# Pruned attention in one core of a Trainium2: the last scaling of the layer norm moved from VectorE to GpSimd, behind the root that is computed there

## The reference

```python
def _layernorm(x, axis=-1, eps=1e-05):
    m = jnp.mean(x, axis=axis, keepdims=True)
    v = jnp.var(x, axis=axis, keepdims=True)
    return (x - m) / jnp.sqrt(v + eps)

def _pruned_attention(q, k, v):
    B, H, S, _ = q.shape
    scores = jnp.einsum('bhqd,bhkd->bhqk', q, k) / math.sqrt(D_K)
    scores = jax.nn.softmax(scores, axis=-1)
    keep = int(S * PRUNE_KEEP)
    col_sum = jnp.sum(scores, axis=2)
    _, idx = jax.lax.top_k(col_sum, keep)
    mask = jnp.zeros((B, H, S), scores.dtype).at[jnp.arange(B)[:, None, None], jnp.arange(H)[None, :, None], idx].set(1.0)
    pruned = scores * mask[:, :, None, :]
    return jnp.einsum('bhqk,bhkd->bhqd', pruned, v)
...
x = _layernorm(x + _L0_attn_ref(x, ...))
x = _layernorm(x + _L0_xattn_ref(x, ctx_1024, ctx_1024, ...))
x = _layernorm(x + _L0_ffn_ref(x, ...))
```

## Time and profile before

| what | value |
|---|---|
| three executions | 2188.01, 2197.36, 2202.60 us, median 2197.36 |
| the profiled execution, its own time | 2182.38 us |
| its span, first to last instruction | 2180.6 us |
| granted TensorE clock, mean | 0.933 |
| the stage's loop, batches 2 to 7 | from about 485 us to 970 us of the span |
| the stage's last store | 1023.6 us |

### The profile page before, as it was taken

One profiled execution on the slowest core, in us unless ns is written; L12 is line 12 of the kernel. 1 busy time (PEld: TensorE's weight loads), 2 busy tenths in 40 slices (PEclk: granted clock), 3 DMA queues, 4 the chain that ended last, 5 costly groups with the idle time before them and its releaser, 6 DMA issues. The chain is left out here.

```text
span 2180.6 us, 28641 instructions
## 1 busy us (share of the span) xinstructions
PE 1880.1 (86%) x8625; PEld 1134.5 (52%) x8625; DVE 1300.3 (60%) x3113; ACT 959.1 (44%) x2451; POOL 609.9 (28%) x781
## 2 busy tenths in 40 slices
PE   7794857888888888884697899999879999999997
PEld 5452534444554454551565565666555656566553
DVE  2483437988988988983354121122266677766655
ACT  3231549988888888880232211111123232223220
POOL 2010005555555555551355000100143122211100
PEclk9897988999999999997666999999999999999999
DMA  5523752112112112202622333433321121100000
GB/s 193 231 87 99 248 183 65 46 54 67 56 54 66 55 54 60 61 20 73 203 92 91 98 109 132 138 123 130 107 77 59 34 63 44 30 15 25 10 10 20
DMA packets 166839, 184.51 MB, mean 85 GB/s; under 512 B 19620, under 2 KB 145819, under 8 KB 165696
## 3 DMA queue, kind: packets, MB, share of 16 engines
q1 hardware_dynamic: 159424, 158.57, 22.5%
q0 software_dynamic: 6144, 16.18, 2.4%
q10 hardware_dynamic: 1152, 8.39, 0.9%
HBM read 118.68 MB, written 58.72 MB: 81 GB/s over the span
## 5 line engine op out<-in xcount | busy, mean ns | idle before, releaser
L746 POOL TENSOR_SCALAR xa_probs<-xa_probs,xa_rinv 128x512 f32<-128x512 f32 x512 | 344.6, 692 | 294.6 <-DVE xa_rinv L791 294.6
L911 PE MATMUL xa_ps_t<-xa_ident,xa_probs 128*128 128x128 f32 x2048 | 325.7, 285 | 60.8 <-POOL xa_probs L746 55.0
L764 ACT ACTIVATE xa_probs<-xa_ps_s,xa_nmax 128x512 f32<-128x512 f32 x512 | 351.9, 708 | 25.8 <-DVE xa_nmax L795 25.4
L911 PEld LDWEIGHTS xa_ps_t<-xa_ident,xa_probs 128*128 128x128 f32 x2048 | 232.4, 143 | 240.1 <-POOL xa_probs L746 84.7
L795 DVE TENSOR_REDUCE xa_nmax<-xa_ps_s 128x2 f32<-128x1024 f32 x256 | 307.3, 1201 | 39.5 <-PE xa_ps_s L903 38.0
L681 ACT ACTIVATE xa_probT<-xa_ps_t 128x512 f32<-128x512 f32 x368 | 226.5, 621 | 63.0 <-PE xa_ps_t L911 54.1
L2268 PE MATMUL ta_ps_e<-k_ew,ta_x5T 128*128 128x512 f32 x512 | 244.2, 613 | 1.5 <-DVE ta_acc L2018 1.4
L903 PE MATMUL xa_ps_s<-xa_k,xa_q 96*128 96x512 bf16 x512 | 157.8, 391 | 54.9 <-ACT xa_probs L764 34.5
L2018 DVE SCALAR_TENSOR_TENSOR ta_acc<-ta_ps_e,ta_gate,ta_acc 128x256 f32<-128x256 f32 x256 | 123.5, 482 | 101.7 <-PE ta_ps_e L2268 95.5
L1459 ACT ACTIVATE ex_hid<-ex_ps_g 128x512 f32<-128x512 f32 x64 | 38.2, 598 | 274.1 <-PE ex_ps_u L1561 274.1
L1515 DVE TENSOR_TENSOR ex_hid<-ex_hid,ex_ps_u 128x512 f32<-128x512 f32 x64 | 44.0, 687 | 182.0 <-ACT ex_hid L1459 182.0
(11 more groups left out here) (356 smaller groups left out, 2935.2 us busy)
## 6 DMA issues: line engine op xcount, KB each, us to landing
xa_q<-scratch_qk_parts SPq DMA_DIRECT2D x192, 64.0 KB, 2.2
xa_k<-scratch_qk_parts SPq DMA_DIRECT2D x192, 64.0 KB, 2.2
scratch_buf<-rec_zeros ACTq DMA_DIRECT2D x8, 1024.0 KB, 12.0
k_wg<-in_L_ffn_Wg SPq DMA_DIRECT2D x16, 512.0 KB, 5.8
k_wu<-in_L_ffn_Wu SPq DMA_DIRECT2D x16, 512.0 KB, 6.0
k_wd<-in_L_ffn_Wd SPq DMA_DIRECT2D x16, 512.0 KB, 6.7
ex_xs<-scratch_buf SPq DMA_DIRECT2D x16, 512.0 KB, 4.9
scratch_results<-ex_out SPq DMA_DIRECT2D x16, 512.0 KB, 3.3
```

The source lines that it names most:

```text
L746: ins = pool.tensor_scalar(probs[h % NP][:, t, :], probs[h % NP][:, t, :], rinv[h % 2][:, t:t + 1], 1.0, ALU.mult, ALU.mult)
L764: ins = act.activation(probs[h % NP][:, t, :], ps_s[j][:, t % 2, :], ACT.Exp, bias=nmax[h % 2][:, t:t + 1], accum_out=rsum[h % 2][:, t:t + 1])
L911: ins = pe.transpose(ps_t[t % 2][:, i * P:(i + 1) * P], probs[(h - 2) % NP][:, i, t * P:(t + 1) * P], ident[:, :])
```

## The change

`finish` leaves DVE's queue and stands in POOL's, in the same slot (half 0, slot 2), ahead of the head's scaling of that slot, behind a wait for POOL's own `root`. SP's store waits for a new semaphore `x2_up` that POOL raises, and the counter `ln`, which DVE raised four times a batch, is raised three times. At the end of the stage `finish` stands behind `root` in POOL's queue.

```diff
-            x_ld, x2_st = r.sem("x_ld"), r.sem("x2_st")
+            x_ld, x2_st, x2_up = r.sem("x_ld"), r.sem("x2_st"), r.sem("x2_up")
...
             def store(b):
-                sp.wait_ge(ln, 4 * b + 4)
+                sp.wait_ge(x2_up, b + 1)
                 sp.dma_start(tok(a["x2"][b]), x_in[:, :, :]).then_inc(x2_st, 16)
...
             def root(b):
-                pool.wait_ge(ln, 4 * b + 3)
+                pool.wait_ge(ln, 3 * b + 3)
                 pool.tensor_tensor(rstd[:, :], ve[:, :], mhalf[:, :], ALU.pow).then_inc(rstd_up, 1)
+
+            def finish(b):
+                pool.wait_ge(rstd_up, b + 1)
+                apart(pool, past_pool)
+                for t in range(T):
+                    ins = pool.tensor_scalar(x_in[:, t, :], x_in[:, t, :], mv[:, t, 0:1], rstd[:, t:t + 1], ALU.subtract, ALU.mult)
+                ins.then_inc(x2_up, 1)
...
                     if (u, h) == (0, 1) and since(b, 2):
                         root(b - 2)
+                    if (u, h) == (0, 2) and since(b, 2):
+                        finish(b - 2)
                     if real:
                         pool.wait_ge(rinv_up, n + 1)
...
             root(B - 1)
+            finish(B - 1)
...
                     if (u, h) == (0, 0) and since(b, 2):
                         stats(b - 2)
-                    if (u, h) == (0, 2) and since(b, 2):
-                        finish(b - 2)
-
-            def finish(b):
-                dve.wait_ge(rstd_up, b + 1)
-                for t in range(T):
-                    ins = dve.tensor_scalar(x_in[:, t, :], x_in[:, t, :], mv[:, t, 0:1], rstd[:, t:t + 1], ALU.subtract, ALU.mult)
-                ins.then_inc(ln, 1)
             batches(dve, body)
             stats(B - 1)
-            finish(B - 1)
```

More of the change, by code:

```diff
@@ L833, in stats @@
                 ins.then_inc(ln, 1)
-                dve.wait_ge(ln, 4 * b + 1)
+                dve.wait_ge(ln, 3 * b + 1)
                 apart(dve, past_dve)
@@ L838, in stats @@
                 ins.then_inc(ln, 1)
-                dve.wait_ge(ln, 4 * b + 2)
+                dve.wait_ge(ln, 3 * b + 2)
                 dve.tensor_scalar(ve[:, :], mv[:, :, 1], 1e-5, None, ALU.add).then_inc(ln, 1)
```

## The result

The changed kernel took 2209.72 us (median of 4 runs, 2207.23 to 2224.03); the kernel before took 2193.01 us beside it (4 runs, 2188.01 to 2202.6). The ratio is 1.0092, with a 95% interval of 1.0047 to 1.0138: some 20 us slower, between 10 and 30. The forecast was 2195.6 us in a range of 2185 to 2204, so the change came out on the other side and outside the range.

A forecast was written before the change was run, and what follows sets the result against it. DVE was taken as the fullest engine (91%), with PE's turned sums close behind finish. Six passes at 0.33 us gave -2.0, the stage's end +0.2: -1.8 us, so 2195.6 us against the median 2197.36, range 2185 to 2204.

The forecast's parts named there:

- the gain is 7.95 - 7.62 = 0.33 us a pass: Half 0, DVE up to the copy of the turned sums: without finish it becomes like half 1, 0.33 us less.
- Rival 1: DVE's queue in half 0: the whole finish, 1.30 us a pass, was on the path; 2189.8 us, chance 0.10.
- Rival 2: In the loop, ACT or PE takes the 0.33 us back; only the end counts: 2197.6 us, chance 0.14.
- I take 0.40 each from start to start: POOL's four pieces of finish: 0.40 us each, 1.6 us together.
- The upper bound is the two-tensor form of the same size, 724 ns: POOL's pieces of finish cost at most 724 ns each, 2.9 us for four.
- the prediction's sum: Loop gain of 2.0 us less 0.2 us added at the stage's end: -1.8 us in all.
- Even at the upper bound, 499.0, it is late by no more than 0.1 us: Half 0, slot 2: POOL's idle 3.22 us covers finish, so head 2's scaling is at most 0.1 us late.
- rival 3: Half 0, slot 2: POOL's finish delays head 2's scaling if pieces exceed 0.79 us; 2205.6 us, chance 0.08.
- Its own formula: Cost at d us a piece: six times 4d - 3.16 in the loop, once 4d - 1.36 at the stage's end.
- POOL has costly forms: POOL's root takes 1.02 us for four columns; at 1.02 a piece, finish would cost +8.2 us together.
- the prediction's twofold price: POOL at twice DVE's time: four pieces take 2.8 us, 1.2 us lost at the stage's end, 2196.8 us.
- d = 1.51 us, twice the dearest row: Price of one POOL piece needed to lose 22 us, over 1% slower; chance 0.03.

The follow-up runs named there:

- the quick form: Changed kernel with finish on POOL as (x + n) * rstd, n = -mean from one more small DVE instruction: 2191.76 us, ratio 1.0007.
- the spread one: Changed kernel with one subtracting piece of finish in each of half 0's slots 2 to 5, last batch's finish on DVE: 2185.54 us, ratio 0.9962.
- The isolated forms: Kernel before with ten TENSOR_SCALAR forms, four of each, in POOL's queue at the program's start, where nothing waits: 2184.35 us, one execution.

## Why the prediction was wrong

**The bound was read rightly.** DVE's 1.30 us in the queue were worth a third of a microsecond: PE's turned sums stood right behind. The step "the gain is 7.95 - 7.62 = 0.33 us a pass" measured 0.32 in each of six passes, in the changed kernel, in the quick form and in the spread one. Rival 1, the whole `finish` on the path, is out: the wait of DVE that would be absent is there, with 0.88 us. Rival 2 is out as well: nothing took the 0.32 back; gaps 3 and on in the quick form are as before, but for 0.2 us at gap 7 where a low stretch lay in one of the two.

**The step that failed** is the price on POOL: "I take 0.40 each from start to start", and with it "The upper bound is the two-tensor form of the same size, 724 ns". It measured 1.21. The bound rested on rows of the same instruction, or of the same size, but none of them subtracted: the scaling multiplies. The isolated forms put all of the difference on the subtraction (1216 against 552 ns with the same operands). With a form that has no subtraction 2.17 us for four was measured, 0.54 each: inside the bounds, and the prediction's sum then holds (-0.9 us worked out, 1.0007 measured). With 1.21 the next step went too: "Even at the upper bound, 499.0, it is late by no more than 0.1 us" became a lateness of 1.60 us, and the scaling of head 2 was released by nothing but POOL's own queue, which the prediction had named as the sign of rival 3.

**Rival 3 happened**, with the mechanism, place and deciding point that it was given, at a chance of 0.08. It needed more than 0.79 us a piece. Its own formula with 1.21 gives 6 x (4.84 - 3.16) = 10.1 us in the loop and 4.84 - 1.36 = 3.5 at the end, 13.6 together. Measured in the profiles: 6 x (1.51 - 0.32) = 7.1 and 3.6. The end is right within 0.1; POOL's own semaphore cost 0.21 us there, not the 0.06 that was taken from the earlier trace rows. The loop is smaller, 1.19 in place of 1.68 a pass: POOL's scaling starts 7.51 - 5.91 = 1.60 us later than before, measured from head 1's, and 1.19 of it is left a gap later. The formula let all of it through; 0.4 us was taken up behind it. In batch 3, where the clock stayed up, DVE waited 1.18 us for the scores behind the late turn (at 591.58), and before it had come to them without a wait (at 586.01).

The row that argued for it was named in the prediction: POOL's `root` at 1.02 us for four columns, "POOL has costly forms". I set it aside because a subtraction is no power. That was an argument from arithmetic, not a measurement, and it carried the whole chance.

**The Trainium skill**, page "GPSIMD Engine Reference", section 4.1 "Engine selection", was weighed in the prediction: VectorE preferred for elementwise work, GpSimd some two times slower with two inputs and near line rate with one. `finish` has one tensor as input, so the prediction's twofold price was not the page's for it. The rule's direction was right. Its sizes agree with no subtracting form here: 4.84 us against DVE's 1.38 is 3.5 times, and the multiply's 0.48 us beside the subtraction's 1.15 to 1.22, all with one tensor as input, shows that the number of inputs doesn't settle it.

**What no rival had** is the clock. I counted a stall of PE at its length. The table above puts 13.8 of the 27.8 us between the two profiles on stretches at 1.2 GHz, less whatever the profile of before had by luck: it lay 10.6 us below its median. That is how the change came to cost some 20 us and not the 10.8 of its own structure. Rival 3's formula gives 13.6 at the measured price, nearer to the 20, but by luck: its loop term is too large by 3 us, and it has no clock. The chance of 0.03 for over 1% slower went by "d = 1.51 us, twice the dearest row"; 1.21 was enough to come to 0.9%.

**The form of the range.** 2185 to 2204 left out rival 3 at its own price of 2205.6, because its chance seemed small. With a cost that no row shows, the upper end should have gone to the dearest row of that engine, not to the dearest of what I held to be alike.

**What stays open.** That a late head brings falls of the clock is shown (head 2 of half 0 and slot 4 of half 1, with the same form of `finish` late and not late). Why it falls in some passes at the stall and in others 20 us later, at the change of halves, isn't settled. Twenty turns in the stall left it to fall later and took hardly any of the loss away, so the idling in the stall is not needed for the later fall. PE's two waits right ahead of that later place were filled by no run, and the kernel before has them as well. Nor is it shown why the spread version gains 8 us where its gaps show 1.9.

## What to carry to other kernels

Price an operation that moves to another engine by a row of that very operation there; the same instruction with another operation can be 2.2 times as dear, and where no such row exists, put four of them into an idle stretch of the queue and read it. If the receiving engine has several idle stretches, give each a piece smaller than the idle time instead of one stretch the sum: with the last `finish` on DVE in both, the same pieces lost 0.8% together and won 0.4% spread. And count a new stall of TensorE at more than its length; here 1.5 us of lateness a pass cost another 1.9 to 2.6 where the clock fell.

## What the runs showed of the hardware that was not expected

- On POOL a TENSOR_SCALAR whose operations include a subtraction took 1.15 to 1.22 us for 128x256 in f32, one of multiplications, or of a multiplication and an addition, 0.48 to 0.56 (add before multiply in the quick form: 2.17 us for four). At 512 columns subtract and multiply by two columns takes 2.09 against 0.71 for the multiplication by a column and a constant, at 64 columns 0.61 against 0.35. The form with the subtraction thus has about 3.3 ns a column against 0.8.
- DVE took the same subtract-and-multiply in 407 ns with four in 1.38 us.
- The granted clock of TensorE halved at an idle time of 2.85 us in some passes of one execution and not in others; at 4.05 us it did in all six. Where it fell, the same four turns took 1.11 us in place of 0.66.
- The clock also fell some 20 us behind such a late head in 27 of 36 passes, against 5 of 48 without one. PE had idled 0.68 and 0.85 us just ahead of that place, as it does in the kernel before. 20 turns that filled the stall, and turns or matmuls in seven slots that left those two waits open, didn't prevent it.
- What a low stretch costs goes by where it falls: in the loop it was 0.2 us at most at gaps 6 and 7, 1 to 2 at the seam of two passes, 1.9 at gaps 8 and 9, and 1.6 to 2.6 at a late head.
